# A two-layer graph network on one core: the loads of edge records move from SyncE's queue to ScalarE's, two per window, into four buffers

## What is computed

```python
# block 1: three graph convolutions, ELU behind each
out_norm, in_norm = rsqrt(max(out_degree, 1)), rsqrt(max(in_degree, 1))
for W, b in ((W0, b0), (W1, b1), (W2, b2)):
    h = h * out_norm[:, None]
    agg = segment_sum(h[src], dst, num_segments=12500) * in_norm[:, None]
    h = elu(agg @ W + b)
x = layernorm(x + h)
# block 2: messages from nodes and edge attributes, then an MLP
msg = relu(x[src] + edge_attr_16 @ W_edge.T + b_edge)
h = (x + segment_sum(msg, dst, 12500)) @ W1.T + b1
h = relu(gamma * (h - mean) * rsqrt(var + 1e-5) + beta)      # over nodes
x = layernorm(x + h @ W2.T + b2)
```

## Time and profile before

| | us |
|---|---|
| median of 3 runs | 7608.19 |
| lowest, highest | 7603.3, 7616.36 |
| span of the profiled execution | 7586.7 |
| of it: windows 1 to 60 of the dense stage | 2170.9 |
| windows 61 to 73 | 427.5 |
| window 74 (half a window) | 82.3 |

### The profile page before, as it was taken

One profiled execution on the slowest core, in us unless ns is written; L12 is line 12 of the kernel. 1 busy time (PEld: TensorE's weight loads), 2 busy tenths in 40 slices (PEclk: granted clock), 3 DMA queues, 4 the chain that ended last, 5 costly groups with the idle time before them and its releaser, 6 DMA issues.

```text
span 7586.7 us, 112214 instructions
## 1 busy us (share of the span) xinstructions
PE 5556.9 (73%) x39907; PEld 3224.8 (43%) x39908; DVE 4274.3 (56%) x14548; ACT 2271.1 (30%) x4057; POOL 3774.9 (50%) x3824
## 2 busy tenths in 40 slices
PE   6599799997777777778777774666766666665666
PEld 5366566665433333333433332333433333333334
DVE  5488888899533333333444112666666665555556
ACT  2487688873100000000001111333333322222223
POOL 4323233354354544545554556565655666665663
PEclk9799899999888988888888886888888888878887
DMA  2333333331555655556556661111111111111111
GB/s 99 140 130 119 120 142 137 118 118 64 177 173 188 197 177 180 186 186 195 184 185 193 218 207 41 32 34 33 33 33 33 34 33 32 33 33 32 32 32 34
DMA packets 438341, 828.25 MB, mean 109 GB/s; under 512 B 161611, under 2 KB 266983, under 8 KB 430951
## 3 DMA queue, kind: packets, MB, share of 16 engines
q1 hardware_dynamic: 305430, 713.88, 27.9%
q0 software_dynamic: 117952, 81.54, 5.1%
q10 hardware_dynamic: 14400, 25.61, 1.2%
HBM read 621.34 MB, written 199.35 MB: 108 GB/s over the span
## 4 chain that ended last, share of the span: by engine, by line
PE 24%; another core or an unknown queue 14%; issue 13%; DVE 11%; PEld 2%; ACT 1%; PEldq 0%; DVEq 0%; ACTq 0%
PE banks L2182 10%; PE banks L2344 4%; DVE tmp L1673 4%; PE banks L2271 2%; PE banks L2304 2%; PEld banks L2182 2%; DVE onehot L1660 2%; DVE rows_f L1652 2%; PE banks L2324 2%; PE banks L2331 1%; PE banks L2164 1%; DVE rows_f L1680 1%; DVE rows_f L1665 1%; PE banks L2157 1%
## 5 line engine op out<-in xcount | busy, mean ns | idle before, releaser
L1086 POOL DMA_INDIRECT rows_f<-table,src_key x1725 | 1708.4, 990 | 1103.4 <-DVE rows_f L1652 604.3
L1051 POOL DMA_INDIRECT sorted_recs<-onehot,rows x1280 | 1235.5, 965 | 1260.6 <-DMA onehot<-edge_recs_dram 718.7
L2182 PE MATMUL banks<-wide,rows_f 128*128 128x512 fp8e4 (+1 forms) x4900 | 1268.1, 400 | 355.4 <-issue 352.3
L1867 ACT ACTIVATE wide<-banks 128x784 fp8e4<-128x784 f32 x1563 | 1205.6, 825 | 484.6 <-PE banks L2104 340.6
L1006 POOL DMA_INDIRECT onehot<-edge_runs_dram,rows_f x472 | 596.2, 1263 | 1149.1 <-DVE onehot L1196 935.9
L2104 PE MATMUL banks<-rows_f 128*128 128x196 f16 (+2 forms) x7525 | 1004.1, 258 | 223.6 <-ACT wide L1867 138.7
L2104 PEld LDWEIGHTS banks<-rows_f 128*128 128x128 f16 x7525 | 708.5, 152 | 612.1 <-ACT wide L1867 401.9
L2271 PE MATMUL banks<-w_edge_blk,rows 80*128 80x320 f32 x690 | 337.4, 578 | 762.9 <-DVE rows_f L1652 521.6
L1444 DVE SCALAR_TENSOR_TENSOR onehot<-banks,onehot 128x98 f16<-128x98 f32 (+2 forms) x1113 | 295.6, 266 | 989.9 <-PE banks L2164 504.1
L1342 DVE TENSOR_TENSOR rows_f<-hid 128x1024 f16<-128x1024 f16 (+1 forms) x1016 | 679.4, 669 | 300.8 <-PE banks L2104 169.5
L1645 DVE TENSOR_SCALAR rows_f<-banks,iota_p 128x512 f16<-128x512 f32 x294 | 220.7, 751 | 1067.0 <-remote 638.8
(11 more groups left out here) (345 smaller groups left out, 7312.1 us busy)
## 6 DMA issues: line engine op xcount, KB each, us to landing
wide<-counts SPq DMA_DIRECT2D x504, 896.0 KB
counts<-wide SPq DMA_DIRECT2D x50, 3136.0 KB
rows_f<-table,src_key POOLq DMA_INDIRECT x1725
sorted_recs<-onehot,rows POOLq DMA_INDIRECT x1280
sorted_recs<-rows SPq DMA_DIRECT2D x28, 640.0 KB
rows<-attr_dram SPq DMA_DIRECT2D x345, 40.0 KB
onehot<-edge_recs_dram SPq DMA_DIRECT2D x143, 90.0 KB
agg_a<-attr_dram ACTq DMA_DIRECT2D x50, 250.0 KB
```

The costliest lines, as they stand in the source:

```text
L1051: G.indirect_dma_start(out=sorted_recs[:, :], out_offset=bass.IndirectOffsetOnAxis(ap=keys_of(t, t + 1).bitcast(I32), axis=0), in_=taken[g ...
L1086: G.indirect_dma_start(out=g_rows[:, n % ROW_RING, k, :], out_offset=None, in_=table32[:, :], in_offset=bass.IndirectOffsetOnAxis(ap=src_k ...
L1867: A.activation(win_counts[o.half % 2][:, :, d0:d0 + o.quads * QUAD].rearrange("p b (q c) -> p b q c", c=QUAD), counted, ACT.Copy, scale=UN ...
L2182: last = M(acc_d[m % 2].rearrange("p (h d) -> p h d", h=2)[:, 0:h, :], layer_rows[n][:, block, :], pieces[:, PLACE[k], 0:h, c * HALF:(c + ...
```

## The change

ScalarE issues the takes instead of SyncE. There are four buffers in place of two (`TAKEN`): the two new ones lie in cells that earlier steps used, so ScalarE waits once, behind window 0, for `s_flagsum` and for the stores of the counts. Takes 0 and 1 are issued ahead of window 0, takes 2 and 3 behind ScalarE's work on it, and behind its work on window m (the exponential; in the last layer the square root) as many as bring the number up to 4 + 1.93 m, rounded up (`TAKES_A_WINDOW`). That is two takes behind each window up to window 71, with one behind windows 15, 29, 43, 58 and 72, and none after that. Take g waits for the puts of granule g - 4. SyncE's queue keeps the pieces and the stores.

```diff
-TAKE_EVERY = 3.75
+TAKEN = 4
+TAKES_A_WINDOW = 1.93
...
-        taken = [onehot_cols(at, GRAN * RECORD).rearrange("p (t r) -> p t r", r=RECORD) for at in (TEMP + (hots + 2) * BLOCKS, FREE + P // 2 + 2 * P)]
+        taken_cells = (TEMP + (hots + 2) * BLOCKS, FREE + P // 2 + 2 * P, 0, GRAN * RECORD)
+        taken = [onehot_cols(at, GRAN * RECORD).rearrange("p (t r) -> p t r", r=RECORD) for at in taken_cells]
...
-        s_put, PUT0 = s_near[2:4], [16 * (b - a) for a, b in SETS[2:4]]
-        PUT_END = [PUT0[s] + 16 * GRAN * len(range(s, RANKED // GRAN, 2)) for s in range(2)]
-        s_take, TAKE0 = [s_load, s_w], [32, 16 * (6 * LAYERS + 2 + CHUNK_TILES + 6)]
+        s_put, PUT0 = s_near[2:6], [16 * (b - a) for a, b in SETS[2:6]]
+        PUT_END = [PUT0[s] + 16 * GRAN * len(range(s, RANKED // GRAN, TAKEN)) for s in range(TAKEN)]
+        s_take, W_LOADED = [s_load, s_w, *s_store], 16 * (6 * LAYERS + 2 + CHUNK_TILES + 6)
+        TAKE0 = [32, W_LOADED, 16 * WINDOWS, 16 * WINDOWS]
...
-            sp.wait_ge(s_outdeg, 1)
-            take_records(0)
-            take_records(1)
-            taken_now = 2
             for m, (n, i, w) in enumerate(DENSE):
                 for k in range(PIECES):
                     if m or k >= 3:
                         load_piece(m, k)
-                    if m >= 1 and taken_now < RANKED // GRAN and taken_now * TAKE_EVERY <= (m - 1) * PIECES + k:
-                        take_records(taken_now)
-                        taken_now += 1
                 if n == LAYERS - 1 and i >= 3:
                     store_rows(i - 3)
-            for g in range(taken_now, RANKED // GRAN):
-                take_records(g)
...
+            def take_records(g):
+
+                if g >= TAKEN:
+                    act.wait_ge(s_put[g % TAKEN], PUT0[g % TAKEN] + 16 * GRAN * (g // TAKEN))
+                act.dma_start(taken[g % TAKEN], edge_recs[:, g * GRAN:(g + 1) * GRAN, :]).then_inc(s_take[g % TAKEN], 16)
+
+            act.wait_ge(s_outdeg, 1)
+            take_records(0)
+            take_records(1)
+            taken_now = 2
...
+                if m == 0:
+                    act.wait_ge(s_flagsum, 1)
+                    for s in range(2):
+                        act.wait_ge(s_store[s], 16 * WINDOWS)
+                while taken_now < RANKED // GRAN and taken_now < TAKEN + TAKES_A_WINDOW * m:
+                    take_records(taken_now)
+                    taken_now += 1
```

More of the change, by code:

```diff
@@ L790, in load_piece @@
                              .rearrange("h p n -> p h n")).then_inc(s_piece[k], 16)
[L792 to L796, removed]
             def store_rows(i):
@@ L883, in sorted_edges @@
             def sorted_edges():
-                for s in range(2):
+                for s in range(TAKEN):
                     sp.wait_ge(s_put[s], PUT_END[s])
@@ L1045, in put_records @@
                 for g in range(RANKED // GRAN):
-                    pool.wait_ge(s_take[g % 2], TAKE0[g % 2] + 16 * (g // 2 + 1))
+                    pool.wait_ge(s_take[g % TAKEN], TAKE0[g % TAKEN] + 16 * (g // TAKEN + 1))
                     for n in range(2):
@@ L1051, in put_records @@
                             G.indirect_dma_start(out=sorted_recs[:, :], out_offset=bass.IndirectOffsetOnAxis(ap=keys_of(t, t + 1).bitcast(I32), axis=0),
-                                                 in_=taken[g % 2][:, n * UNIT + k, :], in_offset=None).then_inc(s_put[g % 2], 16)
+                                                 in_=taken[g % TAKEN][:, n * UNIT + k, :], in_offset=None).then_inc(s_put[g % TAKEN], 16)
             rank_tables()
@@ L1293, in feature_tops @@
             def feature_tops():
-                dve.wait_ge(s_w, TAKE0[1])
+                dve.wait_ge(s_w, W_LOADED)
                 for n in range(LAYERS):
@@ L1889, in _ @@
                     A.activation(stat[:, 0, b], stat[:, 2, b], ACT.Sqrt).then_inc(s_ln, 1)
+                if m == 0:
[5 more added lines that the diff above has]
+                    taken_now += 1
+            assert taken_now == RANKED // GRAN
             def sorted_node_windows():
```

## The result

The kernel after takes **7890.65 us** (median of 4 runs, 7851.81 to 7900.65) against 7607.9 of the kernel before (4 runs): a ratio of 1.0361, 95% interval 1.0332 to 1.0389. 7833 was predicted, so the loss is there, and it is larger: 283 us, not 225.

What follows compares the result with a forecast made beforehand. TensorE was taken to nearly stop some 12 us into unbroken runs of GpSimd's indirect DMAs. Terms +210, +82 and -67 gave +225 on 7586.7, 7812 of span; with 21.5 to the median, 7833 us, range 7660 to 7970.

Steps and rivals of the forecast that it cites:

- Rivals 1, 2 and 5: No coupling, 7541 us (0.12); pauses instead of bursts, 7403 us (0.02); moved takes do nothing, 7608 us (0.04).
- The pairs, +210: Windows 1 to 60: takes issued in pairs make unbroken bursts of 20 puts, 40.3 us a window, +210 us.
- Rival 4: Dearer stops: all steady windows in 1 to 60 at 42 to 44 us, total about 7940 to 8029 us; chance 0.18.
- Windows 61 to 73, +82: Windows without rank turns: last-layer pairs merge into 40 puts without a pause, +82 us, with +11 as the other end.
- sign c: Windows 61 to 72: bursts of 40, windows of about 57 and 24 us in turn, or bursts of 20 with 34 each.
- rival 3: Last layer: the pair doesn't merge, so +11 there and +154 in all, 7762 us; chance 0.22.
- The tail, -67: Window 74: no takes run behind the last piece, so it takes 15 us instead of 82.3, -67 us.
- Sign a: From window 8 on, GpSimd's puts stand in bursts of 20, once a window, no longer in tens.
- b: Layers 0 and 1: even windows of 39 to 43 us, each with some 12 us of few matmuls.
- d: Window 74 takes about 15 us, and no take is issued behind the last piece.
- f: The edge stage keeps its 2920 us.
- (e): TensorE's waits in front of the dense stage's matmul stay with "issue" and grow from 417 to some 650 us.

Runs made afterwards that it cites:

- e1: The changed kernel with nine of ten puts left out and small iotas keeping GpSimd busy instead (output not the reference's): 6688.39 us.
- e3: The changed kernel with ten small iotas, some 3 us, on GpSimd behind every ten puts: 7351.74 us, ratio 0.9625 to the kernel before.
- e11: The changed kernel with three small iotas, about 1 us, on GpSimd behind every five puts: 7260.34 us, ratio 0.9344 to the kernel before.
- e2: The kernel before, with SyncE issuing two takes behind every 7.5 pieces in place of one behind every 3.75: 7848.84 us, ratio 1.029.
- e10: The changed kernel without the drain behind each window, on a chip with stops: 7924.77 us, ratio 1.0198 to the kernel before.
- e4: The kernel before with some 3 us of small iotas on GpSimd behind every ten puts: 7363.46 us, ratio 0.9638.
- e9: The changed kernel as it is, on a chip without stops: 5909.19 us, ratio 0.9961 to the kernel before.

## Why the prediction was right, and where it was off

**The mechanism** was right on chips like the one whose trace it was read from: e1 took the puts away, e3 and e11 the length of their runs, and e2 brought the long runs back alone. Rivals 1, 2 and 5 are out there. Where TensorE "comes nearly to a stop" 12 us into a run, the kernel after shows the same (first 10 us 62 matmuls, next 15.3 us 16).

**The pairs, +210, came out at +317.** This term is the one that was mis-sized, by its price: 40.3 us for a window with a long burst. 46 windows with one burst of 20 took 42.7 us in the mean. The 40.3 was a mean over windows in which the burst lay anywhere; the change puts it at the same place each time, and in layers 0 and 1 that is the window's end, where a drain in the stop holds all of TensorE (14.8 us of idle time for 12.8). 2.0 us times the 49 bursts of 20 are 98 of the 107 us that were missing. The table of e10 says why: 37 of 49 bursts have the window's end in the stop, where it was 6 of 21 before; at the prices of the kernel before (15.2 and 11.9 us) that share alone makes 14.4 us a burst in place of 12.8. The cross-check is in the same trace: in windows 52 to 59 the pair goes out behind the square root, the burst begins 36 us into the window and meets the drain no more; its bursts of 20 cost 10 to 11 us, and the windows take 40 to 43, 41.0 in the mean. Rival 4 named a dearer stop at a fixed place, and its +300 to +406 holds the measured +317, but its reason was the clock. The clock fell (0.80 for 0.87), and TensorE's busy time grew by only 17.5 us. (Its lower end is worked out wrongly: +300 + 82 - 67 gives 7923, not 7940.)

**Windows 61 to 73, +82, came out at +58.** Bursts did merge to 40, in 3 places and not 6 (sign c half right). Two stretches of the kernel after: the 19.4 us from the start of a burst to the first stop where no rank turns are, and 30 us within a burst of 40:

```profile
4485.10:4504.50 19.40, 18.31 (x83) 8.13 (x81) 4.36 (x10) 1.87 (x2) 14.82 (x16) 0.96 0.86 290
4543.30:4573.30 30.00, 7.19 (x13) 1.35 (x13) 0.61 (x2) 0.00 (x0) 22.68 (x25) 0.52 0.16 41
```

The window with a merged burst takes 58 to 60 us (57 was expected), but then one burst of 20 follows alone, with 31 to 34, so that the pattern has three windows and not two. The "2 us in the working" on which rival 3 hung decide it anew each time; in window 65 two bursts of 20 missed each other by 2.8 us (52.6 us).

**The tail, -67, came out at -64.8.** The last take went out at 4939.6 us and its puts reached into window 74, which took 17.5 us, not 15. ScalarE's issues were cheaper than the 0.467 us of SyncE's that stood in for them, and none stands behind the last piece:

```profile
L1867 ACTq DMA_DIRECT2D onehot<-edge_recs_dram x143: 334/335/1383, 1928.9 to 4939.6; - x143
```

**The rest.** Sign a held (20 puts once a window), b held in form but at 42 to 44.6 us, d and f held; the waits in front of L2188 grew to 622.6 us (e), and another 206.8 us of the same stood in front of the rank turns, which the sign didn't count. The 13.5 us by which window 1 starts earlier look like scatter: window 0 starts at 1959.8 us before, 1947.6 after, and between 1948.8 and 1964.1 us in e1 to e4, without order. That 7833 came within 58 us of the median is in part luck: against the +107 of windows 1 to 60 stand -24 of windows 61 to 73, these -13.5, and 18 us by which the profiled execution lay nearer to its median than the one before.

**What the prediction could not see** is that its base was a property of a chip. By the rule of the Trainium skill that it names beside the first edit (DMA: Bandwidth & Descriptors, "Issuing engines are not separate DMA queues") the body of the dense stage would not move. On chips without stops the whole is within 0.4% (e9; no trace of the kernel before shows the body there); on the others e2 shows that what moved it was the grouping of the takes, not the engine that issues them.

## What to carry over

Where one engine stops and no record names a releaser, line the stops up with the bursts of other engines, and price a burst by its place as well as by its length: the same burst costs more where it meets a drain. Then time both kernels on more than one chip before a few per cent are believed; here the sign of the change hangs on the chip (+3.6% on one, -0.4% on another). Where GpSimd must issue many indirect DMAs beside TensorE and stops are seen, 1 us without a DMA behind every five is cheap (-6.6%), but only where GpSimd isn't the bound (+5.0%).

## What was new about the hardware

- On the first chip, the kernel after has TensorE do about 122 instructions (62 matmuls and 60 weight loads, 10.0 us) beside a run of indirect DMAs with rank turns between, or 164 (83 and 81, 19.4 us) without them, and then 13 matmuls in 30 us. Nine of ten puts away, it does so no more (e1: 19 us idle in 1466). In e9, on a chip without stops, it does 64 to 68 matmuls per 10 us beside puts without a pause.
- The kernel before takes 7607.9 to 7758.8 us in three groups of runs and 5931.0 to 5937.6 in two, 22 to 24% less; the edge stage of the kernel after takes 2924.2 us on the first chip and 2297.9 in e9.
- A drain on TensorE is 3.0 us in the median where nothing is stopped (e9), up to 24 where stops are (before). A burst of 20 puts costs 2 to 3.3 us more of TensorE's time when a drain falls into its stop.
- On the chips with stops, two thirds and more of the landing records are missing while puts run (5.0 of some 16 a transfer in the kernel after), and next to none once the puts are gone (e1).
